# Row maxima of three attentions read from PSUM two neighbouring banks at a time

## The chip, the cores and the metric

The kernel runs on one core of a Trainium2 chip. The metric is device time in microseconds (us), lower is better. Three timed runs of the kernel before gave 356.26, 356.95 and 357.55 us.

## What is computed

Two transformer layers over x of shape (4, 256, 128), with 16 heads of 8 dimensions, and mixture-of-experts feed-forward parts. Cut to what matters here:

```python
x = x + attention0(layernorm(x), ctx)        # 256 queries, 64 context keys
x = x + ffn0(layernorm(x))                   # 8 experts, top 2 by weight, and a shared one
n = layernorm(x)
a = layernorm(n + relu(attention1(n, n, n) @ Wo1 + bo1))    # causal, 256 keys
c = relu(attention2(ctx, ctx, a) @ Wo2 + bo2)               # 64 context keys
c = layernorm(c + c)
x = x + layernorm(c + relu(c @ Wf + bf))
x = x + ffn1(layernorm(x))                   # top expert of 8 (the last adds nothing), and a shared one
# each attention: softmax(scale * (Q K^T)) V, per head
```

## The kernel before

**Tiles and stages.** The 1024 tokens are worked in two groups (g = 0, 1), each of two batches b (b = 0, 1 in group 0; b = 2, 3 in group 1) and 512 tokens. The two groups go through the same stages, interleaved on the engines: attention 0, the first feed-forward part, attention 1, attention 2, the second feed-forward part. Steps are tuples such as `("max", a, b, u)`: kind, attention a, batch b, unit u.

**Softmax with its maxima.** The scores are computed twice. First with queries on the partitions: step `max` (L849 to L880 on TensorE) multiplies into one PSUM bank of 128x512 fp32, and VectorE's TENSOR_REDUCE (L1337) takes the maximum over the keys of each head into `MX`. In attentions 0 and 2 a unit is half of a query tile (8 heads of 64 keys, two matmuls, L861): 4 units a batch. In attention 1 a unit is two matmuls (the scores, L871 or L875, and the causal mask added, L878): 4 units of 4 heads x 128 keys for the first query tile, and 8 units of 2 heads x 256 keys for the second: 12 a batch. So there are 4 x (4 + 12 + 4) = 80 units. When all units of a batch are read, step `negmax` negates and splits the maxima on VectorE (L1344, L1345), TensorE transposes them (L885), ScalarE copies them (L1108). Only then may that batch's `scores` begin: they are computed again with keys on the partitions, the negated maxima are added by a matmul (L902, L911), and ScalarE's Exp runs twice for each unit, to fp32 (`pr`, L1117) and to fp16 (`prh`, L1121). The low part `prl` = pr - prh is made on VectorE and GpSimd by turns (steps `plow` and `plow_pool`, both L636), and `pv` multiplies high and low parts with the values (L776 to L778) into a bank kept per group (6 or 7).

**Other steps named later.** `square` is a projection of one group with its work on VectorE after it: `v1` makes the values of attention 1 (VectorE L1372, L1373; first needed by that group's first `pv`), `o0`, `o1`, `o2` are the output projections (VectorE L1369; L1375 and L1376; L1378 and L1379), `f` the dense layer (L1381, L1382). `nat` and `stack` make queries and keys (VectorE L1252; TensorE L825, L826), `kblocks` lays out keys (L1278), `turn` is a transpose (L837, L1261), and the layer norms are L1292, L1295, L1310, L1324 with a power on GpSimd (L726, L727). L1221 splits weights, L1359 normalises an attention's output, L1490 and L1518 belong to the second feed-forward part.

**Banks.** Six PSUM banks (0 to 5) are shared by all steps but the accumulators. Before TensorE writes into a bank, `take` (L763) makes it wait for the bank's last reader.

**Order.** `schedule()` (L283) is a list scheduler that runs when the program is built. It holds an estimated time for each part of a step (`parts`), picks the step that can start soonest and, among those that can start at that same moment, the one with the highest urgency: the longest path behind it, less `GROUP_LEAD` for group 1, plus a number for its kind from `PRESSING` (L335). It also hands each step the free bank or banks that came free first (L337). The result is a fixed order for each engine, and every engine runs its list strictly in order; waits between engines are semaphores.

## Time and profile before

| | |
|---|---|
| timed runs | 356.26, 356.95, 357.55 us; median 356.95 us |
| the profiled execution | 356.45 us, of which the profile's span is 354.4 us; 2.05 us lie around it |
| mean granted TensorE clock over the span | 0.906 |
| steps `max` | 80 on TensorE, 80 reads by VectorE |

The span runs from the first to the last instruction of the profiled execution. A busy share says how much of a stretch an engine had an instruction running. TensorE's instructions overlap and their ends are modelled, so a high share means that it was never long without work, not that it ran at its peak. The granted clock is 1.00 at 2.4 GHz; a stretch at 0.50 ran at 1.2 GHz.

### The profile page before, as it was taken

The page shows a single profiled execution, that of the slowest core. Times are in us where ns is not written, and L with a number is a line of the kernel's source. Part 1 is how long each engine was busy: PE and PEld are TensorE (multiplying, and loading weights), DVE is VectorE, ACT ScalarE, POOL GpSimd, SP SyncE. Part 2 cuts the span into 40 slices and gives each one's busy share as a digit, 9 for nine tenths or more (in the row PEclk, how much of TensorE's full clock was granted, in tenths as well). Part 3 has the DMA queues.
Part 4 walks back from the last instruction along what each step waited for, and adds up shares of the span by engine and source line. Part 5 has one row for each costly group of instructions (what it writes and reads, how often), then busy time and mean ns, then how long its engine had stood idle before and what let it go on. Part 6 is the DMA issues. An engine that isn't in the chain of part 4 may idle for free.

```text
span 354.4 us, 8691 instructions
## 1 busy us (share of the span) xinstructions
PE 283.8 (80%) x3349; PEld 210.3 (59%) x3349; DVE 279.7 (79%) x726; ACT 205.7 (58%) x431; POOL 156.7 (44%) x157
## 2 busy tenths in 40 slices
PE   0396864549999977999997988574797999979994
PEld 0154653424566733787775866433564799758993
DVE  4889999796745589689899557878779998897732
ACT  1464873334757444898886689431873558735561
POOL 9904669653653030344544334411431567442541
PEclk9999995556999989999999899766679999999999
DMA  8502022432020000000000000000003102040030
GB/s 249 227 1 91 13 79 91 130 138 91 15 112 0 0 2 1 3 2 2 4 2 1 2 3 2 2 0 0 2 2 139 42 2 93 2 178 2 18 107 30
DMA packets 6592, 16.62 MB, mean 47 GB/s; under 512 B 660, under 2 KB 2968, under 8 KB 6552
## 3 DMA queue, kind: packets, MB, share of 16 engines
q1 hardware_dynamic: 6552, 16.08, 12.9%
q8 instruction: 27, 0.44, 0.5%
q14 instruction: 13, 0.11, 0.1%
HBM read 10.83 MB, written 0.52 MB: 32 GB/s over the span
## 4 chain that ended last, share of the span: by engine, by line
PE 42%; DVE 34%; ACT 9%; POOL 7%; issue 7%; POOLq 0%; DVEq 0%; ACTq 0%
DVE MX L1337 6%; PE ps L985 5%; PE ps L776 5%; PE ps L777 5%; PE ps L778 5%; DVE prl L636 4%; PE ps L837 2%; ACT pr L1117 2%; DVE stat L1292 2%; ACT prh L1121 2%; ACT lnx L1163 2%; DVE pr L1518 2%; PE ps L973 2%; PE ps L909 1%; PE ps L825 1%
## 5 line engine op out<-in xcount | busy, mean ns | idle before, releaser
L636 POOL TENSOR_TENSOR prl<-pr,prh 128x384 f16<-128x384 f32 (+1 forms) x48 | 49.9, 1042 | 73.9 <-ACT prh L1121 73.9
L1117 ACT ACTIVATE pr<-ps 128x384 f32<-128x384 f32 (+1 forms) x96 | 51.7, 538 | 21.9 <-DVE prl L636 8.9
L1337 DVE TENSOR_REDUCE MX<-ps 128x8 f32<-128x512 f32 (+2 forms) x80 | 52.0, 681 | 8.5 <-PE ps L861 4.1
L1121 ACT ACTIVATE prh<-ps 128x384 f16<-128x384 f32 (+1 forms) x96 | 51.7, 538 | 0.3 <-PE ps L778 0.2
L642 POOL TENSOR_TENSOR prl<-pr,prh 128x512 f16<-128x512 f32 x28 | 33.5, 1205 | 41.1 <-ACT prh L1156 41.1
L745 POOL TENSOR_TENSOR wl<-wraw,wh 128x512 f16<-128x512 f32 (+1 forms) x30 | 35.2, 1198 | 29.3 <-DVE wh L1221 29.2
L636 DVE TENSOR_TENSOR prl<-pr,prh 128x384 f16<-128x384 f32 (+1 forms) x48 | 33.4, 695 | 8.0 <-ACT prh L1121 7.8
L1156 ACT CAST prh<-pr 128x512 f16<-128x512 f32 x28 | 17.2, 618 | 15.0 <-DVE pr L1518 14.8
L837 PE MATMUL ps<-cst,lnx 128*128 128x128 f32 x64 | 15.2, 383 | 12.8 <-DVE lnx L1359 9.9
L1518 DVE TENSOR_TENSOR pr<-ps,hr 128x512 f32<-128x512 f32 x28 | 18.9, 683 | 8.2 <-ACT hr L1150 7.9
L776 PE MATMUL ps<-VSh,prh 128*128 128x9 f16 x192 | 20.5, 169 | 3.7 <-POOL prl L636 3.3
L1150 ACT ACTIVATE hr<-ps 128x512 f32<-128x512 f32 x28 | 16.5, 596 | 9.8 <-PE ps L778 8.9
L776 PEld LDWEIGHTS ps<-VSh,prh 128*128 128x128 f16 x192 | 16.5, 96 | 9.1 <-POOL prl L636 5.6
L726 POOL TENSOR_SCALAR rstd<-mv 128x4 f32<-128x4 f32 x14 | 3.8, 273 | 39.6 <-DVE mv L1295 39.5
L778 PE MATMUL ps<-VSh,prl 128*128 128x9 f16 x192 | 20.1, 167 | 0.0
L777 PE MATMUL ps<-VSl,prh 128*128 128x9 f16 x192 | 20.1, 167 | 0.0
L837 PEld LDWEIGHTS ps<-cst,lnx 128*128 128x128 f32 x64 | 10.3, 195 | 15.8 <-DVE lnx L1359 10.4
L776 PE MATMUL ps<-VBXh,prh 128*128 128x18 f16 x128 | 12.8, 174 | 8.3 <-POOL prl L636 4.4
L778 PE MATMUL ps<-xs,wl 128*128 128x128 f16 x112 | 19.3, 219 | 0.0
L776 PE MATMUL ps<-xs,wh 128*128 128x128 f16 x112 | 19.3, 219 | 0.0
L777 PE MATMUL ps<-xs,wh 128*128 128x128 f16 x112 | 19.3, 219 | 0.0
L1105 ACT CAST tH<-ps 128x512 f16<-128x512 f32 x14 | 8.2, 586 | 17.9 <-PE ps L837 17.9
(256 smaller groups left out, 1058.4 us busy)
## 6 DMA issues: line engine op xcount, KB each, us to landing
wraw<-in_weights SPq DMA_DIRECT2D x8, 768.0 KB, 4.0
wraw<-wh SPq DMA_DIRECT2D x6, 384.0 KB, 2.6
wraw<-wl SPq DMA_DIRECT2D x6, 384.0 KB, 3.0
wraw<-in_weights SPq DMA_DIRECT2D x2, 576.0 KB, 7.3
rowb<-in_rows SPq DMA_DIRECT2D x1, 708.0 KB, 5.2
wd<-in_down SPq DMA_DIRECT2D x1, 576.0 KB, 7.4
X<-in_x SPq DMA_DIRECT2D x1, 512.0 KB, 5.2
picks<-in_spread SPq DMA_DIRECT2D x1, 512.0 KB, 6.0
```

Source lines behind the costliest of these rows:

```text
L636: return engine.tensor_tensor(prl[:, g, three, 0:width], pr[:, g, buffer[("scores",) + e[1:]], 0:width], prh[:, g, three, 0:width], ALU.su ...
L642: return engine.tensor_tensor(hlo[:, g, k % NPV, :], hh[:, g, k % 2, :], hhi[:, g, k % NPV, :], ALU.subtract)
L745: nc.gpsimd.tensor_tensor(wl[:, cols], wraw[:, i % 2, first:end], wh[:, cols], ALU.subtract).then_inc(w_ready, 1)
L776: nc.tensor.matmul(o, a[0], b[0], start=start, stop=False, **kw)
L777: nc.tensor.matmul(o, a[0], b[1], start=False, stop=False, **kw)
L778: return nc.tensor.matmul(o, a[1], b[0], start=False, stop=stop, **kw)
L837: mm = nc.tensor.transpose(o[:, t * P:(t + 1) * P], src[:, g, t, :], ident)
L985: mm = nc.tensor.matmul(o[:, tt], hid0[g][k % NPV][:, tt], w, start=(k == 0 and t == 0), stop=(k == E0 - 1), skip_group_check=True)
L1117: nc.scalar.activation(pr[:, g, buffer[e], 0:width], src[:, 0:width], ACT.Exp, scale=SCALE[a]).then_inc(pr_ready, 1)
L1121: nc.scalar.activation(prh[:, g, buffer3[e[1:]], 0:width], src[:, 0:width], ACT.Exp, scale=SCALE[a]).then_inc(prh_ready, 1)
L1337: nc.vector.tensor_reduce(o, src[:].rearrange("p (h k) -> p h k", h=heads), AX_X, ALU.max).then_inc(max_read, 1)
L1518: nc.vector.tensor_tensor(hh[:, g, k % 2, :], src[:], hr[:, g, k % 2, :], ALU.mult).then_inc(hid_ready[1], 1)
```

## The change

A step `max` now fills two neighbouring banks and VectorE reads both by one TENSOR_REDUCE over 1024 columns. In attentions 0 and 2 a unit is a whole query tile (16 heads, 4 matmuls; 2 units a batch); in attention 1 it is 8 heads x 128 keys (2 units) or 4 heads x 256 keys (4 units), each with 4 matmuls. TensorE's matmuls are the same in number and shape. TensorE now waits for both banks before the first of them and tells VectorE once, after the last. The scheduler looks for two free banks b and b + 1, the pair whose later one came free first; its estimate of the VectorE part becomes 1.23 for a pair (0.68 for one bank before). The eight banks become slices of one PSUM tensor.

The scheduler's priorities change too, so that the whole order is made anew: `GROUP_LEAD` goes from 1.1 to 0, and 26 of the numbers in `PRESSING` change. The largest changes are those left standing in the diff below (and `add1`, which goes from -540 to -1053): `square` goes from 744 to -328, from near the top to below `max` and `scores` (108), `pv` (253) and `plow` (962).

```diff
--- before.py
+++ after.py
@@ -48,12 +48,13 @@
 USED = [4 * P, E0 * P, 9 * P] + [PIECE] * E1
 
 LAST = {0: 3, 1: 15, 2: 3}
-GROUP_LEAD = 1.1
+MAXES = {0: 2, 1: 6, 2: 2}
+GROUP_LEAD = 0
 TABLE_LOAD = 1.3
 LOAD = 5.0
 ARRIVES = {"ctx": 4.5, ("split", 0): 5.5, "split": 14.0, ("ln_stats", "x0"): 8.0, "bo_add": 10.0, "kbs_zero": 7.0}
 
-PRESSING = {... 'ctx': 136, 'kbs_zero': -574, 'ln_center': 235, 'nat': 745, 'negmax': 1082, 'sort_low': 38, 'square': 744, ...}
+PRESSING = {... 'ctx': -215, 'kbs_zero': -103, 'ln_center': 21, 'nat': 1053, 'negmax': 1118, 'sort_low': 287, 'square': -328, ...}
 SHARED = 6
 HOP = 0.17
 
@@ -99,7 +100,7 @@
                 before = [chain([("kblocks", 1, b)], *before)]
                 if b >= 2:
                     also(("kblocks", 1, b), ("scores", 1, b - 2, 15))
-            before = [chain([("max", a, b, u) for u in range(12 if a == 1 else 4)] + [("negmax", a, b)], *before)]
+            before = [chain([("max", a, b, u) for u in range(MAXES[a])] + [("negmax", a, b)], *before)]
             line += [(a, b, u) for u in range(LAST[a] + 1)]
         for i, s in enumerate(line):
             chain([("scores", *s), plow(*s), ("pv", *s)])
@@ -229,7 +230,7 @@
     if k == "scores":
         return [("pe", .46), ("act", .9 if e[1] == 1 else 1.12)]
     if k == "max":
-        return [("pe", .43 if e[1] == 1 else .22), ("dve", .68)]
+        return [("pe", .86 if e[1] == 1 else .43), ("dve", 1.23)]
     if k == "split":
         return [("dve", 1.1 if e[1] else 1.1)]
     if k == "ln_norm":
@@ -274,9 +275,9 @@
 
 def banks_of(e):
 
-    if e[0] == "up1" or e[0] == "up0" and e[2]:
+    if e[0] in ("up1", "max") or e[0] == "up0" and e[2]:
         return 2
-    return int(e[0] in ("max", "scores", "up0", "ctx", "vctx", "nat", "stack", "turn", "square", "negmax", "gate0", "gate1",
+    return int(e[0] in ("scores", "up0", "ctx", "vctx", "nat", "stack", "turn", "square", "negmax", "gate0", "gate1",
                         "spread", "rank", "sort_high", "sort_low", "spots", "downr"))
 
 
@@ -337,6 +338,9 @@
     def banks(e):
 
         known = [b for b in range(SHARED) if b not in holder or holder[b] in end]
+        if e[0] == "max":
+            pairs = [(max(end[holder[c]] if c in holder else 0.0 for c in (b, b + 1)), b) for b in known if b + 1 in known]
+            return [min(pairs)[1], min(pairs)[1] + 1] if pairs else []
         return sorted(known, key=lambda b: end[holder[b]] if b in holder else 0.0)[:banks_of(e)]
 
     def other_table(e):
@@ -545,7 +549,8 @@
         onehot_t = route[:].rearrange("p (s k) -> p s k", s=TILES)
         hid0 = [[pr[:, g, 0, :], pr[:, g, 1, :], prh[:, g, 0:2, :].rearrange("p a k -> p (a k)").bitcast(F32)] for g in range(G)]
 
-        ps = [stk.enter_context(nc.psum_tensor(f"ps{i}", [P, GT], F32)) for i in range(8)]
+        whole_psum = stk.enter_context(nc.psum_tensor("ps", [P, 8, GT], F32))
+        ps = [whole_psum[:, i, :] for i in range(8)]
 
         in_ctx, in_cst, in_x, in_small = sem("in_ctx"), sem("in_cst"), sem("in_x"), sem("in_small")
         in_w, in_wd0, out_done = [sem("in_w0"), sem("in_w1")], sem("in_wd0"), sem("out_done")
@@ -849,16 +854,16 @@
                 elif kind == "max":
                     _, a, b, u = e
                     g = b // 2
-                    take(bank[e][0], max_read, n)
+                    for one in bank[e]:
+                        take(one, max_read, n)
                     q0 = (b % 2) * S
                     if a != 1:
                         if u == 0:
                             pe.wait_ge(stack_ready, nth[("stack", f"q{a}", g, QUADS - 1)])
                             pe.wait_ge(kb_ready, nth[("kblocks", a, 0)])
-                        qt, half = u // 2, u % 2
-                        for i in range(2):
-                            j = 2 * half + i
-                            mm = nc.tensor.matmul(o[:, i * S:(i + 1) * S], QS[:, g, j, q0 + qt * P:q0 + (qt + 1) * P],
+                        for j in range(QUADS):
+                            mm = nc.tensor.matmul(ps[bank[e][j // 2]][:, (j % 2) * S:(j % 2 + 1) * S],
+                                                  QS[:, g, j, q0 + u * P:q0 + (u + 1) * P],
                                                   KBX[:, j, b, :, :].rearrange("p h k -> p (h k)"), start=True, stop=True)
                     else:
                         if u == 0:
@@ -866,17 +871,18 @@
                             pe.wait_ge(const_ready, 5)
                             pe.wait_ge(stack_ready, nth[("stack", "q1", g, QUADS - 1)])
                         kb = kbs[:, b % 2]
-                        if u < 4:
-                            v, heads = o[:].rearrange("p (h k) -> p h k", h=4), 4
-                            nc.tensor.matmul(v, QS[:, g, u, q0:q0 + P], kb[:, u, :, 0:P], start=True, stop=True)
-                        else:
-                            j, h0 = (u - 4) // 2, 2 * ((u - 4) % 2)
-                            v, heads = o[:].rearrange("p (h k) -> p h k", h=2), 2
-                            nc.tensor.matmul(v, QS[:, g, j, q0 + P:q0 + 2 * P], kb[:, j, h0:h0 + 2, :], start=True,
-                                             stop=True)
-                            v = v[:, :, P:2 * P]
-                        mm = nc.tensor.matmul(v, identb[:], trib[:, 0, :].unsqueeze(1).broadcast_to([P, heads, P]),
-                                              start=False, stop=True, skip_group_check=True)
+                        for i, one in enumerate(bank[e]):
+                            if u < 2:
+                                v, heads = ps[one].rearrange("p (h k) -> p h k", h=4), 4
+                                nc.tensor.matmul(v, QS[:, g, 2 * u + i, q0:q0 + P], kb[:, 2 * u + i, :, 0:P], start=True,
+                                                 stop=True)
+                            else:
+                                v, heads = ps[one].rearrange("p (h k) -> p h k", h=2), 2
+                                nc.tensor.matmul(v, QS[:, g, u - 2, q0 + P:q0 + 2 * P], kb[:, u - 2, 2 * i:2 * i + 2, :],
+                                                 start=True, stop=True)
+                                v = v[:, :, P:2 * P]
+                            mm = nc.tensor.matmul(v, identb[:], trib[:, 0, :].unsqueeze(1).broadcast_to([P, heads, P]),
+                                                  start=False, stop=True, skip_group_check=True)
                     mm.then_inc(max_mm, 1)
                 elif kind == "negmax":
                     pe.wait_ge(neg_ready, n)
@@ -1328,17 +1334,18 @@
                 elif kind == "max":
                     _, a, b, u = e
                     dve.wait_ge(max_mm, n)
+                    b0 = bank[e][0]
                     if a != 1:
-                        o, heads = MX[:, b, u // 2, 8 * (u % 2):8 * (u % 2) + 8], 8
-                    elif u < 4:
-                        o, heads = MX[:, b, 0, 4 * u:4 * u + 4], 4
+                        o, heads = MX[:, b, u, :], 16
+                    elif u < 2:
+                        o, heads = MX[:, b, 0, 8 * u:8 * u + 8], 8
                     else:
-                        o, heads = MX[:, b, 1, 2 * (u - 4):2 * (u - 4) + 2], 2
-                    nc.vector.tensor_reduce(o, src[:].rearrange("p (h k) -> p h k", h=heads), AX_X,
-                                            ALU.max).then_inc(max_read, 1)
+                        o, heads = MX[:, b, 1, 4 * (u - 2):4 * (u - 2) + 4], 4
+                    two = whole_psum[:, b0:b0 + 2, :].rearrange("p n c -> p (n c)").rearrange("p (h k) -> p h k", h=heads)
+                    nc.vector.tensor_reduce(o, two, AX_X, ALU.max).then_inc(max_read, 1)
                 elif kind == "negmax":
                     _, a, b = e
-                    dve.wait_ge(max_read, nth[("max", a, b, 11 if a == 1 else 3)])
+                    dve.wait_ge(max_read, nth[("max", a, b, MAXES[a] - 1)])
                     dve.wait_ge(zeroed, 10)
 
                     link(nc.vector.tensor_scalar(MP[:, b, :, 0:H], MX[:, b], -1.0, None, ALU.mult))
```

## Rows read from the trace of the kernel before

**Rows 1.** Page, parts 1 and 4: busy time by engine; the chain's shares by engine and line.
```profile
PE 283.8 (80%) x3349; PEld 210.3 (59%) x3349; DVE 279.7 (79%) x726; ACT 205.7 (58%) x431; POOL 156.7 (44%) x157
PE 42%; DVE 34%; ACT 9%; POOL 7%; issue 7%; POOLq 0%; DVEq 0%; ACTq 0%
DVE MX L1337 6%; PE ps L985 5%; PE ps L776 5%; PE ps L777 5%; PE ps L778 5%; DVE prl L636 4%; PE ps L837 2%; ACT pr L1117 2%; DVE stat L1292 2%; ACT prh L1121 2%; ACT lnx L1163 2%; DVE pr L1518 2%; PE ps L973 2%; PE ps L909 1%; PE ps L825 1%
```
**Rows 2.** Windows of the attentions: stretch, its length, busy us by engine, granted clock.
```profile
26.00:56.00 30.00, 21.18 (x297) 15.96 (x296) 29.48 (x51) 20.33 (x42) 18.35 (x16) 0.94 0.16 54
124.00:140.00 16.00, 12.31 (x63) 5.41 (x60) 14.64 (x36) 7.50 (x16) 2.73 (x3) 0.89 0.00 1
140.00:177.00 37.00, 35.59 (x573) 28.56 (x574) 31.29 (x61) 31.32 (x76) 15.91 (x17) 1.00 0.01 2
177.00:197.00 20.00, 16.97 (x261) 12.69 (x259) 19.40 (x47) 13.05 (x32) 7.81 (x10) 0.97 0.01 3
197.00:217.00 20.00, 18.41 (x273) 14.45 (x273) 12.20 (x22) 17.27 (x42) 7.39 (x8) 0.95 0.01 2
217.00:255.00 38.00, 24.10 (x259) 16.96 (x260) 31.29 (x99) 18.21 (x37) 11.34 (x13) 0.76 0.00 1
```
**Rows 3.** Lines by form, VectorE: shapes, count, busy us, mean ns, idle before, releaser.
```profile
L1337 DVE TENSOR_REDUCE MX<-ps 128x8 f32<-128x512 f32 x32 | 20.8, 682 | 4.2 <-PE ps L861 4.1
L1337 DVE TENSOR_REDUCE MX<-ps 128x2 f32<-128x512 f32 x32 | 20.6, 680 | 0.9 <-PE ps L878 0.9
L1337 DVE TENSOR_REDUCE MX<-ps 128x4 f32<-128x512 f32 x16 | 10.8, 683 | 3.3 <-PE ps L878 3.2
L1490 DVE TENSOR_TENSOR act<-ps,act 128x128 f16<-128x128 f32 x20 | 5.5, 282 | 4.5 <-ACT act L1183 4.3
```
**Rows 4.** Timeline of VectorE, attention 0: start, us, what (merged).
```profile
26.85 3.07 DVE L1337 TENSOR_REDUCE MX<-ps 128x8 f32<-128x512 f32 x5
```
**Rows 5.** Timeline of VectorE, opening of attention 1.
```profile
128.41 0.69 DVE L1337 TENSOR_REDUCE MX<-ps 128x4 f32<-128x512 f32 x1 [0.49 <-PE ps L878]
...
130.97 1.89 DVE L1337 TENSOR_REDUCE MX<-ps 128x4 f32<-128x512 f32 x3 [0.15 <-PE ps L878]
...
135.76 0.69 DVE L1372 CAST VSh<-ps 128x512 f16<-128x512 f32 x1
...
137.21 1.88 DVE L1337 TENSOR_REDUCE MX<-ps 128x2 f32<-128x512 f32 x3
```
**Rows 6.** Timeline of TensorE, the same stretch and the first scores.
```profile
137.33 0.38 PE L825 MATMUL ps<-tH,picks 128*128 128x512 f16 x1 [0.75 <-DVE VSl L1373]
...
139.60 0.29 PE L885 MATMUL ps<-identb,MP 128*128 128x128 bf16 x2 [0.82 <-DVE MP L1345]
140.34 0.38 PE L825 MATMUL ps<-tH,picks 128*128 128x512 f16 x1 [0.46 <-issue]
```
**Rows 7.** Timeline of VectorE, batch 0 of attention 2.
```profile
207.34 0.69 DVE L1337 TENSOR_REDUCE MX<-ps 128x8 f32<-128x512 f32 x1 [1.07 <-PE ps L861]
208.51 0.69 DVE L1337 TENSOR_REDUCE MX<-ps 128x8 f32<-128x512 f32 x1 [0.49 <-PE ps L861]
```
**Rows 8.** Chain of waits, 239 to 256 us: start, us, engine, what.
```profile
242.49 0.61 DVE act L1381
243.12 0.70 DVE act L1382
243.85 0.69 DVE MX L1337
...
248.47 0.69 DVE MX L1337
```
**Rows 9.** Timeline of TensorE: the wait for group 1's maxima in attention 2.
```profile
246.11 0.39 PE L885 MATMUL ps<-identb,MP 128*128 128x128 bf16 x2 [3.91 <-DVE MP L1345]
```
**Rows 10.** Line L1337: idle of VectorE before it until, us in total, times.
```profile
  PE ps L861: 4.1, 5
  PE ps L878: 4.1, 8
```

More of the change, by code:

```diff
@@ L54 @@
 ARRIVES = {"ctx": 4.5, ("split", 0): 5.5, "split": 14.0, ("ln_stats", "x0"): 8.0, "bo_add": 10.0, "kbs_zero": 7.0}
-PRESSING = {'add0': 214, 'add1': -540, 'b3_add': -124, 'back': 211, 'bias': 104, 'bo_add': -101, 'ctx': 136, 'down0': 130, 'down1': -346, 'downr': 1609, 'gate0': 359, 'gate1': 878, 'hi1': -17, 'kblocks': 1011, 'kbs_zero': -574, 'ln_center': 235, 'ln_norm': -42, 'ln_plain': 882, 'ln_pow': 694, 'ln_stats': 695, 'lo1': 990, 'masks0': -180, 'masks1': 13, 'max': 108, 'nat': 745, 'negmax': 1082, 'onehot': -128, 'onehot_t': -914, 'out_norm': 871, 'plow': 962, 'plow_pool': -340, 'pv': 253, 'rank': 1267, 'scores': 108, 'sort_high': -100, 'sort_low': 38, 'split': -31, 'split_low': -1573, 'spots': -649, 'spread': 1033, 'square': 744, 'stack': 121, 'turn': 682, 'up0': 150, 'up1': -357, 'vctx': 249, 'xsplit': -146}
+PRESSING = {'add0': 214, 'add1': -1053, 'b3_add': -124, 'back': 211, 'bias': 39, 'bo_add': -206, 'ctx': -215, 'down0': 130, 'down1': -338, 'downr': 1609, 'gate0': 395, 'gate1': 878, 'hi1': -20, 'kblocks': 1011, 'kbs_zero': -103, 'ln_center': 21, 'ln_norm': -42, 'ln_plain': 884, 'ln_pow': 694, 'ln_stats': 711, 'lo1': 990, 'masks0': -180, 'masks1': 19, 'max': 108, 'nat': 1053, 'negmax': 1118, 'onehot': -131, 'onehot_t': -961, 'out_norm': 871, 'plow': 962, 'plow_pool': -340, 'pv': 253, 'rank': 1252, 'scores': 108, 'sort_high': -87, 'sort_low': 287, 'split': -69, 'split_low': -1630, 'spots': -649, 'spread': 1012, 'square': -328, 'stack': 121, 'turn': 697, 'up0': 157, 'up1': -355, 'vctx': 249, 'xsplit': -146}
 SHARED = 6
```

## The prediction

> **What bounds the kernel now.** I read the page's busy shares and its chain first, then busy times by window around the maxima, then the forms of line L1337, and last the timelines of the places where a maximum stands on the chain. VectorE is busy 79% of the span and TensorE 80%; line L1337 is the costliest single line of the chain, 6% of it, about 21 us [rows 1]. But the windows show different limits [rows 2]. Attention 0 (26 to 56 us) is VectorE's: 29.48 of 30.00 us busy. The opening of attention 1 (124 to 140 us) belongs to VectorE and the hand-over between it and TensorE (14.64 and 12.31 of 16). In the long middle of attention 1 (140 to 177 us) TensorE is busy 35.59 of 37.00 at a granted clock of 1.00 and VectorE has 5.7 us to spare. From 177 to 197 us VectorE is full again (19.40 of 20.00), since group 0's layer norm lies over batch 3's maxima. From 197 to 217 us TensorE and ScalarE lead. From 217 to 255 us VectorE is busy 31.29 of 38.00, most of it in chains of dependent steps, and TensorE waits.
>
> **The reads themselves.** 80 reads of 128x512 take 0.68 us each, the same for 2, 4 or 8 maxima a row [rows 3]; 40 reads of 1024 columns take their place. No row shows a 1024-column read of PSUM. From a 128-column operation out of PSUM (282 ns) to a 512-column one (681 ns) is 399 ns for 384 columns, 1.04 ns a column [rows 3], so 1024 columns come to 681 + 512 x 1.04 = 1214 ns by duration. That looks like 1.36 - 1.21 = 0.15 us saved a pair, 5.9 us over 40. It isn't, because reads overlap: five in a row take 3.07 us [rows 4], so four starts take 3.07 - 0.68 = 2.39, 0.60 us each, and a column still costs 0.53 of it (512 x 1.04). What a joined pair saves in a full queue is 2 x 0.60 - (0.60 + 0.53) = 0.07 us. The bounds are thus 0.15 (each read alone) and 0.07 (queued), or nothing, if a read across a bank edge pays a fresh start. I take 0.07, since the timelines show most reads in runs of two to five [rows 4, 5]: 40 x 0.07 = 2.8 us of VectorE's time at most.
>
> The Trainium skill ("VectorE: DVE Perf Modes", section "The DRAIN you can't avoid") has the next operation wait until the pipeline is empty, and advises to lower the number of operations; by that rule each pair would give back its whole 0.15 us. The five reads at 0.60 us apart [rows 4] speak against it here.
>
> **Attention 0: -0.6 us.** 16 reads become 8, and 8 x 0.07 = 0.6 us come off an engine that is 98% busy [rows 2]. What covers nothing here: VectorE had only 0.5 us idle. The first read isn't late: the five reads from 26.85 on run without a gap [rows 4], so TensorE was ahead. Two banks are now given back together, after 1.2 us and not one after 0.6. Bounds -1.2 and +0.5 (if TensorE then lacks a pair once and VectorE runs dry).
>
> **Opening of attention 1: +0.4 us from the pairs.** TensorE delivers the first units one by one, and VectorE waits 0.49 us for the first and 0.15 to 0.16 for the next three (the first and the last of the four: [rows 5]), so they come 0.86 us apart. A pair can be read only after the second unit: the first read starts 0.86 later, and again waits 0.5 for the second pair (due at 130.97, free at 129.27 + 1.21 = 130.48). Idle grows from 0.49 + 3 x 0.16 = 0.97 to 0.49 + 0.86 + 0.49 = 1.84, that is +0.87; six pairs give back 6 x 0.07 = 0.4. Net +0.4, bounds 0 and +0.9. This is the added wait: in front of the first pair nothing is queued that VectorE could do instead, and negmax, then all scores, stand behind.
>
> **Opening of attention 1: -1.4 us from the new order.** Between the maxima VectorE makes the values of group 1: L1372 starts at 135.76 and the next maxima start at 137.21, so 1.45 us [rows 5]. TensorE meanwhile waits 0.75 us for it, then 0.82 us for the negated maxima, then 0.46 us [rows 6]. Group 1's values are first needed by its first pv, behind both batches of group 0. With `square` at -328 and `max` at 108 they go behind the last maxima, and negmax comes 1.45 us sooner. The cap is TensorE's idle there, 2.0 us, because the middle after it is TensorE's and only idle that is filled here shortens it. I take -1.4; bounds -2.0 and 0 (if the values then stand in front of the first low part instead, or hold TensorE's bank).
>
> **Middle and end of attention 1: -0.4 us.** 36 reads become 18. Twelve pairs (batches 1 and 2) lie in the window where TensorE is 96% busy: nothing. Their cover is TensorE's matmuls, unchanged in number; if it were gone they would give 12 x 0.07 = 0.8. Six pairs (batch 3) lie where VectorE is 97% busy: 6 x 0.07 = 0.4. Bounds -1.3 and +0.5: a max unit now wants two neighbours out of six banks, and TensorE, strictly in order, holds the scores queued behind it while it waits, and ScalarE and GpSimd behind those.
>
> **Attention 2: 0.** Eight pairs give 0.6 in VectorE's queue. Against it, two of the four batches are fed by TensorE one unit at a time, between scores: the reads at 207.34 and 208.51 waited 1.07 and 0.49 us [rows 7]. A pair starts 1.2 us later there and takes 1.21, ending at 208.51 + 1.21, against 208.51 + 0.69 before, 0.5 later, though that window is TensorE's and ScalarE's [rows 2]. Over the whole kernel reads waited 8.2 us for TensorE in 13 places [rows 10]. I take 0, bounds -0.6 and +1.0.
>
> **Square steps of group 0: +0.6 us.** The same demotion puts the VectorE parts of o1, o2 and f behind maxima of the other group. At 242.49 the dense layer's two operations are on the chain with maxima between them and the norm (243.85, 248.47) [rows 8]. A double read in front costs up to 1.2 us where a single one cost 0.6: +0.6, once. The other side of it is that group 1's negated maxima come sooner: TensorE waited 3.91 us for them at 246.11 [rows 9]. Bounds +3.6 (three squares, 1.2 each) and -1.4 (only the gain for group 1, the length of L1381 and L1382). GROUP_LEAD and the other numbers swap ties between steps; I take them at nothing, with 2 us to either side, about the size of the largest single waits at these hand-overs [rows 6, 9].
>
> **The sum.** -0.6 + 0.4 - 1.4 - 0.4 + 0 + 0.6 = -1.4 us. Against the profiled execution's 356.45 us this is 355.05; that execution lies 0.5 us under the median of the timed runs, which would give 355.55. I take the middle, 355.3, and count the rivals from the same 356.7.
>
> **The rivals.**
> - *Covered (no change).* The opening's gain is not kept: VectorE has the values to make before the first low parts anyway, and TensorE's middle runs on as before. Then -0.6 + 0.4 - 0.4 + 0.6 = 0: 356.7. For it: TensorE's work is the same and it is 96% busy for 37 us [rows 2]. Against it: TensorE's 2.0 us idle right before that stretch [rows 6].
> - *Crossing (slower).* The demoted squares of group 0 each wait behind a double read, and its chain of norms sets the start of the second feed-forward part: 3 x 1.2 = 3.6 in place of 0.6, so -1.4 + 3.0 = +1.6, and with another 0.9 if single-fed pairs in attention 2 end on the path (0.5 in batch 0, worked out above, and 0.4 in another): +2.5, 359.2. It decides once two of the three squares meet a read just begun. For it: 217 to 255 us is a chain with maxima of group 1 in it [rows 8]. Against it: VectorE is idle for 6.7 of those 38 us [rows 2], and a square that becomes ready in such a gap is taken at once, whatever its number.
> - *Whole fixed cost comes back.* If two reads in a row did cost their durations, 0.15 a pair, attention 0 gives 1.2 and batch 3 0.9, the opening +0.9 - 0.9 = 0: the sum is -1.2 + 0 - 1.4 - 0.9 - 0.6 + 0.6 = -3.5, 353.2. This is also the time if the new order takes 2 us more of TensorE's 3.91 us wait [rows 9]. The skill's section on the DRAIN, named above, would have it so.
> - *The change doesn't do what it says.* The 1024-column read pays 0.68 twice (at 1.36 us it saves nothing and loses the overlap, 0.16 a pair): VectorE-bound places lose 20 x 0.16 = 3.2 in place of gaining 1.0, so -1.4 + 4.2 = +2.8, 359.5.
>
> **Chances.** Forecast 0.43 (355.3, its own range 354.2 to 355.9); covered 0.24; crossing 0.18; whole cost or more from the order 0.12; not as it says 0.03. About 0.3%, 1.07 us, is what a measurement of this kernel can tell from no change, so faster means under 355.9 and slower over 358.0. Faster is 0.40 of the forecast and 0.11 of the third rival: 0.51. Slower is 0.16 of crossing, 0.03 of the last and 0.03 of covered: 0.22. Same is the rest, 0.27. The range runs from 352.0 (the third rival less 1.2 for the open ties) to 359.5 (crossing and a little of them).
>
> **What the changed profile would show.** 40 reads of 1.21 us, and in runs 1.13 us apart; 1.36 or more would make the last rival right. In the opening of attention 1 the first read about 0.9 us later after kblocks, L1372 of group 1 behind the second operation of negmax, and TensorE's waits before the first scores (2.0 us) mostly gone. In the middle TensorE still over 95% busy and the stretch no shorter. L1375 and L1381 of group 0 with or without a read just before them tells forecast from crossing. The prediction is wrong if the new order moves steps in the feed-forward parts, where I count nothing, or if TensorE stands at L861 or L871 waiting for a pair.

## The result, and the profile after

The changed kernel takes 374.68 us (373.33 to 375.81) beside 357.25 us for the kernel before on the same chip: 1.050 times as long, 95% interval 1.046 to 1.055. The prediction said 355.3 us, a range of 352.0 to 359.5 and a chance of 0.22 for slower. Here and below medians are over all executions and ratios over those within 1.5% of the fastest of their kernel. The changed kernel's profiled execution has a span of 372.3 us, 17.9 more than before, though VectorE does less work. Page of the changed kernel, parts 1 and 4, against [rows 1]:

```profile
PE 292.3 (79%) x3349; PEld 215.8 (58%) x3349; DVE 273.6 (73%) x686; ACT 206.2 (55%) x431; POOL 157.3 (42%) x157
...
PE 55%; DVE 24%; POOL 8%; issue 6%; ACT 5%; DVEq 0%; ACTq 0%; POOLq 0%
PE ps L781 9%; PE ps L783 8%; PE ps L782 8%; PE ps L991 5%; DVE MX L1345 4%; DVE prl L641 4%; PE ps L1053 3%; PE ps L842 3%; PE ps L884 2%; POOL wl L750 2%; PE ps L915 2%; POOL prl L641 2%; PE ps L1083 2%; PE ps L881 2%; PE ps L917 1%
```

VectorE is busy 273.6 us, 6.1 less, and the maxima (now line L1345) fell from 6% to 4% of the chain. So the change did what it says and the time went elsewhere. The reads by form in the changed kernel (lines by form, VectorE), against [rows 3], and the longest run of them (timeline of VectorE), against [rows 4]:

```profile
L1345 DVE TENSOR_REDUCE MX<-ps 128x4 f32<-128x1024 f32 x16 | 19.3, 1219 | 5.1 <-PE ps L884 4.9
L1345 DVE TENSOR_REDUCE MX<-ps 128x16 f32<-128x1024 f32 x16 | 19.2, 1217 | 2.5 <-PE ps L865 2.3
L1345 DVE TENSOR_REDUCE MX<-ps 128x8 f32<-128x1024 f32 x8 | 9.8, 1224 | 7.1 <-PE ps L884 7.1
```
```profile
135.24 3.48 DVE L1345 TENSOR_REDUCE MX<-ps 128x4 f32<-128x1024 f32 x3
```

A read of 1024 columns takes 1.22 us (1.21 was worked out), and three in a row start (3.48 - 1.22) / 2 = 1.13 us apart, as worked out. The idle in front of the reads went from 8.2 us [rows 10] to 14.7. Windows of the changed kernel, against [rows 2]:

```profile
26.00:56.00 30.00, 23.08 (x277) 16.81 (x276) 27.45 (x43) 19.57 (x40) 20.81 (x18) 0.90 0.24 80
124.00:140.00 16.00, 11.91 (x62) 5.74 (x60) 12.97 (x25) 7.50 (x16) 2.52 (x3) 0.89 0.00 1
140.00:177.00 37.00, 33.35 (x468) 24.57 (x468) 29.15 (x40) 24.95 (x60) 12.52 (x13) 0.95 0.01 2
...
255.00:290.00 35.00, 24.41 (x230) 16.43 (x228) 26.93 (x103) 16.87 (x32) 11.09 (x12) 0.74 0.05 20
```

The last of these stretches in the kernel before, which [rows 2] don't have:

```profile
255.00:290.00 35.00, 31.32 (x388) 24.15 (x387) 30.80 (x100) 19.56 (x37) 15.12 (x15) 0.92 0.12 47
```

The long middle of attention 1 shows it: between 140 and 177 us TensorE ran 573 matmuls before and 468 now, and ScalarE's 31.32 busy us became 24.95. And from 255 to 290 us, where group 0's second feed-forward part should be under way, TensorE is busy only 24.41 of 35.00 us at a clock of 0.74 (31.32 at 0.92 before). The lower clock isn't the cause by itself: over its span e4 below was granted 0.910, more than the 0.906 of before, and its span is 367.4 us. Two losses, then. The scores of attention 1 (line L909 before, L915 now) and the output projection o1 of group 0 (L1375 before, L1382 now) place them. Kernel before:

```profile
L909 PE MATMUL ps<-QS,kbs x64: 269/272/422, 140.8 to 211.1; 128*128 128x256 f16 x64
L1375 DVE TENSOR_TENSOR act<-ps,rowb x2: 680/686/691, 181.8 to 223.2; 128x512 f32<-128x512 f32 x2
```

Changed kernel:

```profile
L915 PE MATMUL ps<-QS,kbs x64: 269/272/421, 140.3 to 218.3; 128*128 128x256 f16 x64
L1382 DVE TENSOR_TENSOR act<-ps,rowb x2: 681/686/692, 200.9 to 231.7; 128x512 f32<-128x512 f32 x2
```

The columns are the count, then min/median/max ns, then the starts of the first and the last. The 64 scores start 0.5 us sooner and stretch over 78.0 us in place of 70.3. o1 of group 0 comes 19.1 us later.

**Why the scores stretch.** Timeline of VectorE in the second batch of attention 1, kernel before:

```profile
150.43 0.68 DVE L1337 TENSOR_REDUCE MX<-ps 128x2 f32<-128x512 f32 x1
151.33 0.69 DVE L1337 TENSOR_REDUCE MX<-ps 128x2 f32<-128x512 f32 x1 [0.22 <-PE ps L878]
151.94 0.55 DVE L636 TENSOR_TENSOR prl<-pr,prh 128x384 f16<-128x384 f32 x1
152.41 1.28 DVE L1337 TENSOR_REDUCE MX<-ps 128x2 f32<-128x512 f32 x2
```

Changed kernel, VectorE, and then TensorE filling the banks in the same stretch:

```profile
148.91 1.22 DVE L1345 TENSOR_REDUCE MX<-ps 128x8 f32<-128x1024 f32 x1 [0.74 <-PE ps L884]
...
151.22 1.21 DVE L1345 TENSOR_REDUCE MX<-ps 128x4 f32<-128x1024 f32 x1
...
153.62 1.22 DVE L1345 TENSOR_REDUCE MX<-ps 128x4 f32<-128x1024 f32 x1 [0.72 <-PE ps L884]
154.76 0.55 DVE L641 TENSOR_TENSOR prl<-pr,prh 128x384 f16<-128x384 f32 x1
155.84 1.23 DVE L1345 TENSOR_REDUCE MX<-ps 128x4 f32<-128x1024 f32 x1 [0.53 <-PE ps L884]
```
```profile
150.28 0.38 PE L881 MATMUL ps<-kbs,QS 128*128 128x512 f16 x1 [0.48 <-DVE MX L1345]
150.60 0.38 PE L881 MATMUL ps<-kbs,QS 128*128 128x512 f16 x1
152.77 0.38 PE L881 MATMUL ps<-kbs,QS 128*128 128x512 f16 x1
153.10 0.38 PE L881 MATMUL ps<-kbs,QS 128*128 128x512 f16 x1
154.99 0.38 PE L881 MATMUL ps<-kbs,QS 128*128 128x512 f16 x1
```

Each fill begins just after the read before it has ended: the read of 148.91 ends at 150.13 and the fill begins at 150.28; 152.43 and 152.77; 154.83 and 154.99. Fill and read take turns on one pair of banks, and the pairs follow each other 2.2 to 2.4 us apart. Indeed the kernel's scheduler gives all six pairs of this batch banks 0 and 1, while the scores go around the other four. Before, VectorE read one bank while TensorE filled another.

TensorE itself waits little for these reads. It is VectorE that stands at a pair not yet filled, with the low parts behind it in its list, and for these wait ScalarE and then TensorE. Waits from 140 to 223 us (waited for; us in total, times, longest), kernel before, then changed:

```profile
DVE MX L1337 <- PE ps L878: 3.1, 4, 2.2
ACT pr L1117 <- DVE prl L636: 4.3, 8, 1.5
PE ps L776 <- DVE prl L636: 0.5, 2, 0.3
...
DVE MX L1345 <- PE ps L884: 9.8, 11, 2.0
ACT pr L1123 <- DVE prl L641: 13.0, 12, 2.1
PE ps L781 <- DVE prl L641: 4.9, 7, 1.8
PE ps L881 <- DVE MX L1345: 0.5, 1, 0.5
```

The last line is the only wait of TensorE's matmuls for a read of maxima there. For the changed kernel this path is read from one trace and not tested. In e4, below, the pairs go around more banks, neighbouring pairs of a batch share a bank 6 times of 20 and not 12 times, and there TensorE's matmuls do wait 4.2 us for reads in the same stretch; its scores take as long.

### The profile page after: what moved, and what is told of

It reads as the page before. It is cut to its first block, busy times and chain, and to the rows that moved or that the text cites. A ratio compares the mean times of both kernels' runs of the same rounds, so it can differ in the third digit from the quotient of the medians.

```text
span 372.3 us, 8687 instructions
## 1 busy us (share of the span) xinstructions
PE 292.3 (79%) x3349; PEld 215.8 (58%) x3349; DVE 273.6 (73%) x686; ACT 206.2 (55%) x431; POOL 157.3 (42%) x157
## 4 chain that ended last, share of the span: by engine, by line
PE 55%; DVE 24%; POOL 8%; issue 6%; ACT 5%; DVEq 0%; ACTq 0%; POOLq 0%
PE ps L781 9%; PE ps L783 8%; PE ps L782 8%; PE ps L991 5%; DVE MX L1345 4%; DVE prl L641 4%; PE ps L1053 3%; PE ps L842 3%; PE ps L884 2%; POOL wl L750 2%; PE ps L915 2%; POOL prl L641 2%; PE ps L1083 2%; PE ps L881 2%; PE ps L917 1%
## 5 line engine op out<-in xcount | busy, mean ns | idle before, releaser
L641 POOL TENSOR_TENSOR prl<-pr,prh 128x384 f16<-128x384 f32 (+1 forms) x48 | 50.9, 1061 | 82.4 <-ACT prh L1127 82.4
L1345 DVE TENSOR_REDUCE MX<-ps 128x16 f32<-128x1024 f32 (+2 forms) x40 | 48.1, 1219 | 14.7 <-PE ps L884 11.9
L647 POOL TENSOR_TENSOR prl<-pr,prh 128x512 f16<-128x512 f32 x28 | 32.6, 1172 | 43.6 <-ACT prh L1162 43.6
L641 DVE TENSOR_TENSOR prl<-pr,prh 128x384 f16<-128x384 f32 (+1 forms) x48 | 35.6, 742 | 8.3 <-ACT prh L1127 8.0
L781 PE MATMUL ps<-VSh,prh 128*128 128x9 f16 x192 | 19.7, 170 | 8.7 <-DVE prl L641 6.9
L731 POOL TENSOR_SCALAR rstd<-mv 128x4 f32<-128x4 f32 x14 | 4.9, 352 | 49.3 <-DVE mv L1301 49.1
L781 PE MATMUL ps<-VBXh,prh 128*128 128x18 f16 x128 | 13.1, 175 | 14.9 <-POOL prl L641 6.5
L1156 ACT ACTIVATE hr<-ps 128x512 f32<-128x512 f32 x28 | 16.6, 598 | 14.2 <-PE ps L783 13.4
L781 PEld LDWEIGHTS ps<-VBXh,prh 128*128 128x128 f16 x128 | 10.8, 99 | 18.0 <-POOL prl L641 8.0
L915 PE MATMUL ps<-QS,kbs 128*128 128x256 f16 x64 | 18.5, 288 | 1.5 <-ACT MT L1114 0.7
L783 PE MATMUL ps<-VSh,prl 128*128 128x9 f16 x192 | 19.3, 168 | 0.0
L782 PE MATMUL ps<-VSl,prh 128*128 128x9 f16 x192 | 19.3, 168 | 0.0
```

Source lines behind the costliest of these rows:

```text
L641: return engine.tensor_tensor(prl[:, g, three, 0:width], pr[:, g, buffer[("scores",) + e[1:]], 0:width], prh[:, g, three, 0:width], ALU.su ...
L647: return engine.tensor_tensor(hlo[:, g, k % NPV, :], hh[:, g, k % 2, :], hhi[:, g, k % NPV, :], ALU.subtract)
L781: nc.tensor.matmul(o, a[0], b[0], start=start, stop=False, **kw)
L782: nc.tensor.matmul(o, a[0], b[1], start=False, stop=False, **kw)
L783: return nc.tensor.matmul(o, a[1], b[0], start=False, stop=stop, **kw)
L915: nc.tensor.matmul(o[:, 0:S], kb[:, j, h, 0:P], QS[:, g, j, q0:q0 + S], start=True, stop=True)
```

## The experiments

Two theories went in. **Banks:** a pair costs because it holds two banks and is handed over as one piece. **Order:** the new priorities cost. All ratios are to the kernel before on the same chip.

**e1, e2: the priorities without pairs.** e1 has the new `GROUP_LEAD` and all of `PRESSING`; e2 has one number.

```diff
-PRESSING = {... 'square': 744, ...}
+PRESSING = {... 'square': -328, ...}      # e2; e1: every number of the change, GROUP_LEAD = 0
```

> The kernel before with single-bank reads, but with the changed GROUP_LEAD and PRESSING: the priorities alone. Two theories. BANKS: the loss of 17 us is made by the pairs (in the changed kernel the maxima of a batch of attention 1 go around one pair of banks, one read each 2.2 to 2.5 us, and the 64 scores take 78.0 us in place of 70.3); the priorities are then harmless and this kernel stays within 2 us of before, 355 to 359 us. ORDER: the loss is made by the priorities (o1 of group 0, L1375 before, is read by VectorE at 181.8 us in before and at 200.9 us in the changed kernel, although the attention's out_norm behind it came only 8.5 us later, so 10.6 us of delay are the demoted square's); this kernel then keeps about that, 366 to 370 us.

Measured: 371.16 us, 1.045 (1.039 to 1.051), about 1 us above Order's case.

> The kernel before with one number changed: 'square' from 744 to -328. My prediction counted -1.4 us for the values of group 1 moved out of the opening of attention 1 and +0.6 us for group 0's squares behind maxima: 356.4 us. ORDER: the demoted o1 of group 0 waits behind batch 3's maxima and scores, about 10 us, so 364 to 369 us, and most of e1's loss is here. BANKS: within 2 us of before.

Measured: 370.24 us, 1.041 (1.033 to 1.049), again 1 us above Order's case. One number alone costs 13.4 us, nearly all of what the whole new set does. VectorE reached o1 of group 0 at 193.8 us.

**e3, e4: pairs without the priorities.** e3 lets the scheduler plan pairs with the old numbers. e4 doesn't let it plan at all: it takes the lists of the kernel before, joins each two neighbouring `max` steps where the second stood, and only hands out banks anew.

```diff
-    orders, _, bank = schedule()
+    orders, _, bank = schedule(merged(1))   # e4: forced lists, from single reads with the old numbers
```

> The changed kernel with the GROUP_LEAD and PRESSING of before: pairs alone, with the order made anew from them by the scheduler. BANKS: it is at least as slow as the changed kernel, 372 us or more, since the new priorities were only making the best of the pairs. ORDER: most of the loss goes, 357 to 364 us.

Measured: 396.93 us, 1.115 (1.110 to 1.120).

> Pairs in the order of before: every engine keeps the list of before, each two neighbouring max steps are one (placed where the second stood), and only the banks are handed out anew. This takes the order out of the question. BANKS: in attention 1 a pair is held for its fill and its read (0.65 + 1.22 us and the hand-overs), so attention 1 grows by 8 us or more: 365 to 372 us. ORDER: nothing but my prediction's terms without the order is left, -0.6 + 0.4 - 0.4 = -0.6 us: 355 to 358 us.

Measured: 372.60 us, 1.048 (1.041 to 1.055), 0.6 us above Banks' case. Scores of e4 (its own line numbers), and what VectorE waited for in front of its reads:

```profile
L971 PE MATMUL ps<-QS,kbs x64: 269/272/418, 143.6 to 222.8; 128*128 128x256 f16 x64
```
```profile
L1402 DVE TENSOR_REDUCE MX<-ps x40: 1191/1221/1225, 27.2 to 267.1; 128x16 f32<-128x1024 f32 x16, 128x4 f32<-128x1024 f32 x16, 128x8 f32<-128x1024 f32 x8
its engine sat idle before it (us, times) until:
  PE ps L910: 8.8, 12
  PE ps L891: 6.2, 4
```

With the order of before, pairs cost 15.7 us by themselves, and the 64 scores stretch over 79.2 us. Planned with the old numbers they cost 40. So both theories hold, and neither alone: the priorities cost 14.3 us with single reads (e1) and save 22 us with pairs (396.93 against 374.68). The two losses don't add up (15.7 + 14.3 is 30, and 17.4 was measured).

**e5, e12: where pairs cost.**

> As e4 (pairs in the order of before, 372.6 us), but only the maxima of attention 1 are pairs; attentions 0 and 2 read single banks. BANKS: attention 1 is where scores and maxima of two batches run side by side and share six banks; there TensorE has no idle to hide a late pair in. Nearly all of e4's +15.7 us is here: 369 to 372 us. If the loss were spread by the number of pairs (24 of 40), 366 us; if it came from VectorE being full, attention 0 would carry it and this kernel would be under 362 us.

```diff
-PAIRED = {0, 1, 2}
+PAIRED = {1}
```

Measured: 368.22 us, 1.034 (1.029 to 1.039): +11.5 of e4's +15.7 us, from 24 of 40 pairs. Its scores stretch over 79.2 us like e4's. This is less than "nearly all" and more than a share by the number of pairs (366 us).

> Pairs in attention 0 alone, in the order of before. This is the one place where my prediction found VectorE 98% busy and gave pairs -0.6 us. HOLD (pairs cost by the banks they hold and by joint hand-over): in attention 0 a batch's maxima run mostly by themselves, so little is lost; with the gain 0 to +2 us: 356 to 358 us. My term alone: 355.4 us. Both are near what can be told from no change; clearly over 358 would say that pairs cost in every attention.

Measured with `PAIRED = {0}`: 358.13 us, 1.000 (0.996 to 1.004). Eight pairs in attention 0 are no change that can be measured; a gain of 0.6 us isn't ruled out. This kernel also has all banks as slices of one PSUM tensor, so that part of the change costs nothing that can be measured. What e4 has over e5 and e12, some 4 us, would be the eight pairs of attention 2, if the parts add up; no run has those alone.

**e6, e7, e8: what about a pair costs.** All three have e4's lists. e6 also has its banks, but hands each bank over by itself; e7 keeps e4's joint hand-over and reads the two banks by two instructions; e8 is e7 with any two free banks.

```diff
-                        nc.vector.tensor_reduce(o, two, AX_X, ALU.max).then_inc(max_read, 1)
+                        for i in range(2):                          # e6
+                            dve.wait_ge(max_mm, 2 * n - 1 + i)      # TensorE tells after each bank
+                            nc.vector.tensor_reduce(o[:, i * half:(i + 1) * half], ps[bank[e][i]]..., AX_X,
+                                                    ALU.max).then_inc(max_read, 1)
```

> The order and the banks of e4, but each half of a pair is handed over by itself: TensorE waits for the second bank only before its own matmuls and tells VectorE after each bank, and VectorE reads 512 columns twice, giving each bank back after its read. Only the joint hand-over and the joined read are taken away. If the coarse hand-over makes the loss, this falls back towards before, 357 to 362 us. If it is the position of the steps (both halves at the second's place) and the banks in neighbouring pairs, it stays at 369 to 373 us.

Measured: 365.44 us, 1.025 (1.017 to 1.032), scores over 74.1 us. This is between the two cases: 7.2 of e4's 15.7 us come back with single hand-overs, 8.7 us stay with the place in the lists and the banks. (e4 ran on another chip; against e7 below, on the same one and differing in the hand-over alone, the ratios say 1.025 and 1.046, some 7.5 us.)

> As e4, with the joint hand-over kept (both banks waited for, told once, given back once), but VectorE reads the pair in two instructions of 512 columns. It differs from e4 by the joined read alone, 40 x 0.07 us of VectorE's time: 372 to 375 us. It differs from e6 by the hand-over alone.

Measured: 376.10 us, ratio 1.046 (1.039 to 1.052; its two shortest executions took 371.86 and 373.72 us), the same as e4's ratio within its interval. Joining the read itself neither gains nor loses what can be told here.

> As e7, but the two banks of a step are any two, those that came free first, and need not be neighbours. Against e7 it prices neighbourhood alone. If looking for neighbours makes most of the loss, 358 to 364 us; if holding two banks does, at most 4 us come back: 368 to 372 us.

Measured: 369.03 us, 1.033 (1.028 to 1.039). Against e7's ratio that is 0.012 less, some 4 us for not having to be neighbours (the intervals only just miss each other). Most of the loss is left.

**e11: a bank taken from single reads.**

```diff
-        known = [b for b in range(SHARED) if b not in holder or holder[b] in end]
+        known = [b for b in range(BANKS) if b not in holder or holder[b] in end]     # BANKS = 5; lists of before, as in e4
```

> The kernel before, single reads, the order of before on every engine, but the banks are handed out from five and not six. If holding banks is what pairs cost, then taking one bank away from single reads must cost about as much as pairs in the order of before do (e4, +15.7 us; a pair holds two banks for about 2.4 us in place of two single holds of about 1.2 us, one bank more at any time while maxima run): 366 to 373 us. If banks are plentiful and the hand-over alone makes the loss, under 359 us.

Measured: 366.28 us, 1.025 (1.014 to 1.035), scores over 73.9 us (143.5 to 217.4). So the sixth bank is worth some 9 us, in a kernel whose page nowhere shows a bank as a bound. It is about what stays in e6, and not as much as all of e4's 15.7 us, which the expectation asked for: by this measure holding banks makes a good half of what pairs cost in this order, which leaves the rest to the hand-over.

**e9, e10: the two squares apart.** A number given to one named square is added to that of its kind: 744 - 1072 = -328.

> The kernel before with only the square o1 at -328, all other squares at 744. e2 (all squares demoted) stands at 370.2 us, +13.4, and there o1 of group 0 reached VectorE at 193.8 us (181.8 in before), and every later step of group 0 came 12 us later. If the loss is this one step behind batch 3's maxima and scores, this kernel has 9 to 12 us of the 13.4: 366 to 369 us. If it is several squares, each a little (my crossing rival), it has a third or less: 358 to 361 us.

```diff
-'square': 744
+'square': 744, ('square', 'o1'): -1072      # e10: ('square', 'v1'): -1072
```

Measured: 371.22 us, 1.041 (1.035 to 1.046), 2 us more than expected: o1 alone carries all of e2's loss. Timeline of VectorE in e9, around o1 of group 0:

```profile
178.82 0.55 DVE L636 TENSOR_TENSOR prl<-pr,prh 128x384 f16<-128x384 f32 x1
...
187.22 2.04 DVE L1337 TENSOR_REDUCE MX<-ps 128x2 f32<-128x512 f32 x3
189.17 0.55 DVE L636 TENSOR_TENSOR prl<-pr,prh 128x384 f16<-128x384 f32 x1
189.63 0.17 DVE L1344 TENSOR_SCALAR MP<-MX 128x32 bf16<-128x32 f32 x1
...
191.20 0.68 DVE L1375 TENSOR_TENSOR act<-ps,rowb 128x512 f32<-128x512 f32 x1
```

On VectorE o1 isn't behind one read but behind the whole batch: all the rest of batch 3's maxima and its negmax. But the same number also moves o1's matmuls on TensorE. Their first one in the kernel before, in e9 and in the changed kernel:

```profile
180.90 0.22 PE L776 MATMUL ps<-wh,tH 128*128 128x128 f16 x1
...
190.18 0.22 PE L776 MATMUL ps<-wh,tH 128*128 128x128 f16 x1
...
200.07 0.22 PE L781 MATMUL ps<-wh,tH 128*128 128x128 f16 x1
```

In e9 they start 9.3 us later, right behind the last of batch 2's scores (189.84), and VectorE's o1 starts 9.4 us later, 0.2 us after the last of them has ended. In the changed kernel VectorE even waits 0.79 us for them at 200.94. So TensorE's half alone is late enough to explain o1; no run moves one half without the other.

> The kernel before with only the square v1 at -328. My prediction gave this -1.4 us (the values of group 1, 1.45 us of VectorE, moved from in front of the last maxima of the first batch): 355.5 us. The rival: TensorE's part of v1 moves back too, the first scores come no sooner (in e2 the first scores began at 142.2 us, 140.8 in before), and the time is the same or up to 2 us longer: 357 to 359 us.

Measured: 358.75 us, 1.008 (1.004 to 1.011): slower, where I had -1.4 us. It doesn't add to o1's loss: e9 and e10 together would be 18 us, and e2, which has both, costs 13.4.

**e13: better numbers for pairs.**

> The changed kernel with other numbers in GROUP_LEAD and PRESSING, found by a search that tried several thousand sets and kept the one with the shortest plan of the kernel's own list scheduler (368.2 in its units, 373.2 for the changed kernel, 360.5 for before). HOLD: no order hides the held pairs; this comes to 366 to 370 us, faster than the changed kernel and still some 10 us behind before. If the changed kernel's loss were mainly its priorities, a better set would bring pairs to 357 us or less.

Measured: 376.76 us, 1.051 (1.044 to 1.057), no better than the changed kernel, though its plan was 5 units shorter, and some 7 us above the range expected of it. No version was found that beats the kernel before.

**The chain behind all of them.** The router of the second feed-forward part of group 0 (the maximum over its logits, L1419 before) is the end of group 0's chain of attentions and norms. Its start, the span, and what lies between, from each kernel's profiled execution:

| kernel | 64 scores of attention 1 | o1 of group 0 | router of group 0 | span | span less router |
|---|---|---|---|---|---|
| before | 140.8 to 211.1 | 181.8 | 261.4 | 354.4 | 93.0 |
| changed | 140.3 to 218.3 | 200.9 | 277.7 | 372.3 | 94.6 |
| e1 priorities alone | 144.7 to 213.2 | 194.9 | 275.4 | 368.5 | 93.1 |
| e2 square alone | 142.2 to 211.5 | 193.8 | 273.7 | 368.6 | 94.9 |
| e9 o1 alone | 140.8 to 209.4 | 191.2 | 270.7 | 369.0 | 98.3 |
| e4 pairs, old order | 143.6 to 222.8 | 190.1 | 274.5 | 367.4 | 92.9 |
| e6 single hand-over | 143.0 to 217.1 | 186.3 | 269.8 | 362.7 | 92.9 |
| e11 five banks | 143.5 to 217.4 | 185.9 | 267.6 | 362.9 | 95.3 |

In all of them the end is late by about as much as the router of group 0 (within 2.3 us), except e9, where 5.3 of 14.6 us come after it. Of these, 3.9 come behind the router of group 1 (it starts at 315.2 in e9, with 53.8 us to the end, and at 304.5 before, with 49.9), and e2 also has 53.8 us behind it. Why these tails are longer stays open. In e2 the scores take no longer than before (69.3 us), yet the router is 12.3 us late. In e4 o1 comes 8.3 us late and the router 13.1. Pairs and a demoted o1 work on the same chain, and that is at least one reason why they don't add up.

## Why the prediction was wrong

**The price of a read: right.** 1.21 us and 1.13 us apart were forecast, 1.22 and 1.13 measured. The sentence of the Trainium skill ("VectorE: DVE Perf Modes", section "The DRAIN you can't avoid") that the prediction used would have had starts a full duration apart; the 3.48 us for three reads speak against it again. The same section of the Trainium skill adds what the prediction left out, that an operation that is not held (made to wait until all before it have finished) starts earlier, and 1.13 us between starts at 1.22 us each agrees with that.

**Attention 0, -0.6 us:** not told from nothing (e12).

**Opening, +0.4 and -1.4 us: both failed.** The scores of the changed kernel start 0.5 us sooner, not 1.0. The pairs' term is seen alone in e5, whose keys (kblocks) start when they did before (125.5 and 125.6 us): the first read is 0.9 us late, as forecast, but the negated maxima are 1.0 late and the scores start at 142.6, 1.8 us late, where 0.9 was the bound. As for the order, e10 shows v1's demotion to be a loss of 2.8 us. `v1` is two steps. I looked at group 1's, in the opening [rows 5], and not at group 0's, which the line's own view of the kernel before shows at 119.1 us:

```profile
L1372 DVE CAST VSh<-ps x2: 692/693/694, 119.1 to 135.8; 128x512 f16<-128x512 f32 x2
```

Timeline of VectorE in the changed kernel:

```profile
121.77 0.69 DVE L1517 TENSOR_TENSOR X<-ps,X 128x512 f32<-128x512 f32 x1 [3.74 <-PE ps L991]
...
124.30 0.66 DVE L1379 CAST VSh<-ps 128x512 f16<-128x512 f32 x1
124.99 0.69 DVE L1380 TENSOR_TENSOR VSl<-ps,VSh 128x512 f16<-128x512 f32 x1
...
129.93 1.22 DVE L1345 TENSOR_REDUCE MX<-ps 128x8 f32<-128x1024 f32 x1 [1.82 <-PE ps L884]
```

Demoted too, it ran behind a gap of 3.74 us that it could have filled, in front of the keys and the first maxima. The gain that I had counted is there: from keys to scores e2 takes 14.0 us (128.2 to 142.2) and the kernel before 15.2 (125.6 to 140.8). But its keys start 2.6 us late. A number for a kind moves every step of that kind.

**Middle and end of attention 1, -0.4 us with +0.5 at worst: the first of the two steps that failed most.** With the opening's pairs it measured +11.5 us (e5); 1.8 us of that are there when the scores start. I named the mechanism, a step that wants two of six banks with scores queued behind it, and priced it as one wait, 0.5 us. But it can come back with every pair. The price can be worked out: a fill of 0.65 us (0.33 a bank between 152.77 and 153.10) and a read of 1.21 that may not overlap, and some 0.15 us for a hand-over each way (150.13 to 150.28 above), are 2.16 us a pair, where two queued reads took 1.20. That is up to 0.96 us a pair, 17 us for these 18 pairs, if each one had to wait for the read before it; not all do, and e5's 11.5 us are less. The sentence "their cover is TensorE's matmuls" took TensorE's business as protection. There it was the thing to be protected: its stream of scores is what the late pairs break up (573 matmuls became 468), and by the changed kernel's trace mostly not through a wait of TensorE for a bank, as I had it, but through VectorE's low parts.

**Attention 2, nothing with +1.0 at worst:** not priced alone; what is left of e4's loss, some 4 us, points above the bound.

**Square steps, +0.6 us with +3.6 at worst: right in sign, far off in size, and with half of the step left out.** The crossing rival saw the VectorE parts behind reads and put 1.2 us, one double read, on each square. e9 measured +15.2 us for o1 alone. I didn't ask where TensorE's half of a square goes: its matmuls ended up behind all of batch 2's scores, 9.3 us late. On an engine where work of a higher number is always ready, a lower number doesn't mean behind one step but behind the last of them. My argument against it, that VectorE is idle 6.7 of 38 us from 217 to 255, was taken from the wrong place: o1 of group 0 falls in the stretch before, from 177 to 197 us, where VectorE was 97% busy [rows 2].

**Ties and other numbers, nothing with 2 us to either side:** this held with single reads, where e1 and e2 differ by 0.9 us. With pairs the new numbers, square's among them, save 22 us (e3 against the changed kernel), and no run prices the others apart.

**The scheduler's plan as a forecast.** The list scheduler is part of the kernel, and its plan's length can be read when the program is built. Plan (its units) and measured median of the kernels that have their own plan:

```
before 360.5 356.9 | changed 373.2 374.7 | e1 370.7 371.2 | e2 369.6 370.2 | e3 396.6 396.9 | e4 374.2 372.6
e5 371.3 368.2 | e8 370.6 369.0 | e9 369.9 371.2 | e10 361.1 358.8 | e11 370.7 366.3 | e12 360.8 358.1 | e13 368.2 376.8
```

The prediction didn't use it. Taken as differences from before, the plan has the sign right for every kernel that measures slower, and up to e12 it is too low by at most 6 us (e9: +9.4 planned, +15.2 measured against the 355.99 us of its own chip). For e13, where a search had made the plan short, +7.7 was planned and 19.4 measured: there, used as a target, the plan was no longer a forecast. It also can't tell e6 from e4 and e7, whose order and banks are the same.

**The total** missed because terms of -0.4 us (with the opening's +0.4) and +0.6 us measure 11.5 and 15.2 us on their own. The split of the changed kernel's 17.4 us between them stays open, since they overlap. What the joint hand-over alone costs (7 us of e4's 15.7) and what the neighbourhood costs (some 4) were measured in the order of before only. One read over two banks that aren't neighbours wasn't tried.

## What to carry to other kernels

Price a larger unit by the whole turn of its buffer, fill plus hand-over plus read plus hand-over, times the buffers it holds, and see whether two such turns fit beside what else wants them; the fixed cost that the larger unit saves (here 0.07 us a pair) is usually the small term. Here an engine that was 96% busy, strictly in order, didn't hide its neighbours' waits but passed them on. And where an order is made by a scheduler from numbers for kinds of steps, a change of numbers is to be read step by step along the longest chain: ask of each demoted step, and of each engine that has a part of it, what is always ready in front of it.

## What the runs showed of the hardware that was not expected

A VectorE read over the edge between two PSUM banks costs next to nothing extra: 1217 to 1224 ns for 1024 columns against 681 + 512 x 1.04 = 1214. Nothing else was new; the losses are those of banks and order, and the kernel with five banks in place of six (+2.5%) shows how little of that a page of busy shares tells.
